# Cross-attention scores of two heads on the two row halves of the matmul array

## The reference, cut to what matters

```python
qh = (q @ Wq).reshape(b, l, HEADS, HEAD_DIM).transpose(0, 2, 1, 3)   # 16 heads of 64, l = 128
kh = (kv @ Wk).reshape(b, s, HEADS, HEAD_DIM).transpose(0, 2, 1, 3)  # s = 2048
vh = (kv @ Wv).reshape(b, s, HEADS, HEAD_DIM).transpose(0, 2, 1, 3)
qh = rms_norm(qh, q_norm_w)
kh = rms_norm(kh, k_norm_w)
scores = jnp.einsum('bhld,bhsd->bhls', qh, kh) * (1.0 / np.sqrt(HEAD_DIM))
scores = jnp.where(mask, scores, NEG_INF)
attn = jax.nn.softmax(scores, axis=-1)
o = jnp.einsum('bhls,bhsd->bhld', attn, vh)
```

## Time and profile before

| | us |
|---|---|
| runs shown: median (lowest to highest of 3) | 1441.21 (1439.97 to 1441.74) |
| profiled execution, its own time | 1442.03 |
| its span, first to last instruction | 1440.3 |
| cross attention, from its first context piece (76) to its last output (1002) | about 926 |
| mean granted clock of PE, share of full speed | 0.932 |

### The profile page before, as it was taken

How to read it: one execution, slowest core, us unless ns; L and a number is a source line. 1 busy time by engine, 2 the same in 40 slices (tenths; PEclk the granted TensorE clock), 3 DMA queues, 4 the chain that set the end, 5 groups by cost and what they waited for, 6 DMA issues and landing times. The chain is left out here.

```text
span 1440.3 us, 30819 instructions
## 1 busy us (share of the span) xinstructions
PE 1230.4 (85%) x11696; PEld 1025.7 (71%) x11696; DVE 870.4 (60%) x1880; ACT 743.7 (52%) x1222; POOL 821.5 (57%) x699
## 2 busy tenths in 40 slices
PE   4669999989999999999999999995798855479418
PEld 3548888878888888888888888873587744368316
DVE  5846555576555577555576555553767668587573
ACT  4534666666666667566666666564533331123550
POOL 3516777767777768777767777774501126276210
PEclk9889999999999999999999999996999977779759
DMA  5044667797766798767688767667510022032000
GB/s 177 30 125 85 116 117 120 129 186 130 117 115 118 119 187 155 115 114 119 121 177 144 116 119 121 114 117 152 193 45 1 1 96 88 1 88 59 0 0 30
DMA packets 427554, 149.68 MB, mean 104 GB/s; under 512 B 408208, under 2 KB 408208, under 8 KB 427280
## 3 DMA queue, kind: packets, MB, share of 16 engines
q1 hardware_dynamic: 427408, 147.71, 52.7%
HBM read 45.94 MB, written 1.05 MB: 33 GB/s over the span
## 5 line engine op out<-in xcount | busy, mean ns | idle before, releaser
L358 PE MATMUL pair<-wkv_hi,ctx_hi 128*128 128x256 f16 x2048 | 560.5, 274 | 14.7 <-DVE ctx_lo L541 14.7
L360 PE MATMUL pair<-wkv_hi,ctx_lo 128*128 128x256 f16 x2048 | 560.3, 274 | 0.0
L359 PE MATMUL pair<-wkv_lo,ctx_hi 128*128 128x256 f16 x2048 | 560.3, 274 | 0.0
L566 DVE CUSTOM_DVE_ANT_0 probs<-bank,mask 128x512 f32<-128x512 f32 x256 | 176.7, 690 | 291.3 <-PE bank L636 282.9
L487 POOL TENSOR_TENSOR k_rinv<-k_ms,half_neg 128x8 f32<-128x8 f32 x128 | 212.7, 1662 | 206.3 <-DVE k_ms L585 204.8
L477 POOL TENSOR_TENSOR p_parts<-probs,p_parts 128x512 f16<-128x512 f32 x256 | 291.9, 1158 | 49.2 <-ACT p_parts L522 48.7
L358 PEld LDWEIGHTS pair<-wkv_hi,ctx_hi 128*128 128x128 f16 x2048 | 200.9, 98 | 67.5 <-DVE ctx_lo L541 16.4
L359 PEld LDWEIGHTS pair<-wkv_lo,ctx_hi 128*128 128x128 f16 x2048 | 201.1, 98 | 50.0
L360 PEld LDWEIGHTS pair<-wkv_hi,ctx_lo 128*128 128x128 f16 x2048 | 201.1, 98 | 24.0
L526 ACT ACTIVATE k_lh<-k_n 128x512 f16<-128x512 f32 x128 | 80.5, 629 | 205.8 <-DVE k_n L591 205.2
L515 ACT ACTIVATE probs<-probs,neg_max 128x512 f32<-128x512 f32 x256 | 182.9, 714 | 1.3 <-DVE neg_max L575 1.1
(11 more groups left out here) (244 smaller groups left out, 2048.6 us busy)
## 6 DMA issues: line engine op xcount, KB each, us to landing
ctx_raw<-in_ctx_t_dram SPq DMA_DIRECT2D x64, 256.0 KB, 3.0
cross_out_raw<-in_w_qkv_dram SPq DMA_DIRECT2D x12, 512.0 KB, 4.2
pt<-p_parts SPq DMA_TRANSPOSE x256, 3.3
down_raw<-in_w_down_dram SPq DMA_DIRECT2D x12, 256.0 KB, 2.7
ffn_raw<-in_w_up_dram SPq DMA_DIRECT2D x12, 256.0 KB, 2.8
ffn_raw<-in_w_gate_dram SPq DMA_DIRECT2D x12, 256.0 KB, 2.6
w_raw<-in_wq_dram SPq DMA_DIRECT2D x4, 512.0 KB, 7.9
w_raw<-in_wk_dram SPq DMA_DIRECT2D x4, 512.0 KB, 4.8
```

The source lines that it names most:

```text
L358: nc.tensor.matmul(to, x_hi[k], w_hi[k], start=(k == 0), stop=False)
L359: nc.tensor.matmul(to, x_hi[k], w_lo[k], start=False, stop=False)
L360: mm = nc.tensor.matmul(to, x_lo[k], w_hi[k], start=False, stop=(k == n - 1))
L566: nc.vector.tensor_tensor_reduce(probs[n % PROBS][:, :], scores[:, :], mask[:, k, :], 1.0, LOWEST, ALU.add, ALU.max, chunk_max[head % 2][: ...
```

## The change

**Scores.** A pair of parts (one chunk, both heads) is now scored in one slot, every second slot. The keys of the first head stand on rows 0 to 63 and those of the second on rows 64 to 127, hi in the first half of `kt` and lo in the second; `q_st` is laid out in the same way. Each head takes three products (hi·hi, lo·hi, hi·lo; lo·lo, which was a by-product, is no longer made), each a matmul of 64 rows and 512 columns, the two heads in turn, each into a bank of its own (`bank[4]`, `bank[5]`). PE waits once for each pair until DVE has taken the last scores of both.

**PSUM.** `pair` has two tensors instead of three, so a projection waits for `k_n` and `v_lo` of the projection two before it. The outputs of the two heads have a bank each (`two`).

**Order and buffers.** The parts now alternate between the heads. The lags are 8, 17 and 20 instead of 10, 15 and 18; `kt` has 3 buffers instead of 6, `probs` 10 instead of 6, the small maxima 4 instead of 2.

**Prologue.** `stack` holds hi of eight heads and then lo of eight heads. Eight transposes for each unit, into two banks in turn, and one copy by DVE give `q_st`. The second set of transposes, ACT's copy and DVE's copy `hi2` are gone.

```diff
-SCORE_LAG, EXP_LAG, PV_LAG = 10, 15, 18
-CTX_RAWS, KTS, VS, PROBS, PTS = 2, 6, 11, 6, 3
+SCORE_LAG, EXP_LAG, PV_LAG = 8, 17, 20
+CTX_RAWS, KTS, VS, PROBS, PTS = 2, 3, 11, 10, 3
...
@@ -74,9 +74,11 @@
             of_stage[1].extend(handles)
             return handles
 
-        pair = [whole.enter_context(nc.psum_tensor(f"pair{i}", [P, 4, 256], F32)) for i in range(3)]
-        bank = [pair[i // 2][:, 2 * (i % 2):2 * (i % 2) + 2, :].rearrange("p a n -> p (a n)") for i in range(6)]
-        bank += [whole.enter_context(nc.psum_tensor(f"bank{i}", [P, 512], F32)) for i in (6, 7)]
+        pair = [whole.enter_context(nc.psum_tensor(f"pair{i}", [P, 4, 256], F32)) for i in range(2)]
+        bank = [pair[i // 2][:, 2 * (i % 2):2 * (i % 2) + 2, :].rearrange("p a n -> p (a n)") for i in range(4)]
+        bank += [whole.enter_context(nc.psum_tensor(f"bank{i}", [P, 512], F32)) for i in range(4, 6)]
+        two = whole.enter_context(nc.psum_tensor("two", [P, 2, 512], F32))
+        bank += [two[:, i, :] for i in range(2)]
 
...
-                    pe.wait_ge(hi2_done, m + 1)
-                    wait(pe, st_a, m)
-                    for h in range(HH):
-                        mm = nc.tensor.transpose(t_a[:, h * P:(h + 1) * P],
-                                                 stack[m % 2][:, h, 0:2, :].rearrange("p a d -> p (a d)"), ident16[:, :])
+                    wait(pe, st_a, m - 1)
+                    for i in range(HH):
+                        mm = nc.tensor.transpose(t_a[m % 2][:, i * P:(i + 1) * P],
+                                                 stack[m % 2][:, :, :, :].rearrange("p a h d -> p (a h d)")[:, i * P:(i + 1) * P],
+                                                 ident16[:, :])
                     mm.then_inc(tr_a, 1)
-                    wait(pe, st_b, m)
-                    for h in range(HH):
-                        mm = nc.tensor.transpose(t_b[:, h * P:(h + 1) * P],
-                                                 stack[m % 2][:, h, 1:3, :].rearrange("p a d -> p (a d)"), ident16[:, :])
-                    mm.then_inc(tr_b, 1)
...
-                wait(act, tr_b, m - 1)
-                nc.scalar.activation(stack[m % 2][:, :, 0, :], q_w[m % 2][:, :, :], ACT.Copy).then_inc(hi_done, 1)
-
-            def keep(m):
-                act.wait_ge(tr_b, m + 1)
-                nc.scalar.activation(q_st[:, unit(m)[2], 1, :, :].rearrange("p h q -> p (h q)"), t_b[:, :],
-                                     ACT.Copy).then_inc(st_b, 1)
+                wait(act, tr_a, m - 1)
+                nc.scalar.activation(stack[m % 2][:, 0, :, :], q_w[m % 2][:, :, :], ACT.Copy).then_inc(hi_done, 1)
...
-                wait(dve, tr_b, m - 1)
-                nc.vector.tensor_copy(stack[m % 2][:, :, 2, :], stack[m % 2][:, :, 0, :]).then_inc(hi2_done, 1)
-                nc.vector.tensor_tensor(stack[m % 2][:, :, 1, :], q_w[m % 2][:, :, :], stack[m % 2][:, :, 0, :],
+                nc.vector.tensor_tensor(stack[m % 2][:, 1, :, :], q_w[m % 2][:, :, :], stack[m % 2][:, 0, :, :],
                                         ALU.subtract).then_inc(lo_done, 1)
 
...
-        k_n = sb("k_n", [P, 2, TILES, HD], F32, c)
-        k_lh = [sb(f"k_lh{i}", [P, 2 * TILES, 2, HD], F16, c) for i in range(2)]
-        kt = [sb(f"kt{i}", [P, 2, CHUNK], F16, c) for i in range(KTS)]
+        k_n = sb("k_n", [P, TILES, 2, HD], F32, c)
+        k_lh = [sb(f"k_lh{i}", [P, 2, CHUNK], F16, c) for i in range(2)]
+        kt = [sb(f"kt{i}", [P, 2 * TILES, P], F16, c) for i in range(KTS)]
...
-        pair, scores = g["pair"], bank[6]
-        o_new = bank[7][:, 0:2 * VW].rearrange("p (h v) -> p h v", h=2)
+        pair, scores = g["pair"], bank[4:6]
+        o_new = g["two"][:, :, 0:VW]
...
-            return pair[d % 3][:, :, 0:2 * HD].rearrange("p t (h e) -> p h t e", h=2)
+            return pair[d % 2][:, :, 0:2 * HD].rearrange("p t (h e) -> p t h e", h=2)
 
         def v_of(d):
 
-            return pair[d % 3][:, :, 2 * HD:4 * HD].rearrange("p t (h e) -> p t h e", h=2)
+            return pair[d % 2][:, :, 2 * HD:4 * HD].rearrange("p t (h e) -> p t h e", h=2)
...
-                        wait(pe, k_n_done, d - 2)
-                        wait(pe, v_lo_done, d - 2)
+                        wait(pe, k_n_done, d - 1)
+                        wait(pe, v_lo_done, d - 1)
...
-                        sp.wait_ge(s_done, last_score(d - KTS))
-                    sp.dma_start_transpose(kt[d % KTS][:, :, :].rearrange("p h (t k) -> p (h t) k", t=TILES),
-                                           k_lh[d % 2][:, :, :, :].rearrange("p a b e -> p (a b e)")).then_inc(kt_in[d % 2], 16)
+                        sp.wait_ge(s_done, d - KTS + 1)
...
-                    dve.wait_ge(s_done, n + 1)
+                    dve.wait_ge(s_done, n // 2 + 1)
...
-                if (n := part(SCORE_LAG, slot)) is not None:
-                    u, h, k = n // 8, n // CHUNKS % 2, n % CHUNKS
-                    b, group, at = u // GROUPS, u % GROUPS, CHUNKS * u + k
+                if (n := part(SCORE_LAG, slot)) is not None and n % 2 == 0:
+                    u, at = n // 8, n // 2
+                    b, group = u // GROUPS, u % GROUPS
                     pe.wait_ge(kt_in[at % 2], 16 * (at // 2 + 1))
                     wait(pe, s_max_done, n)
-                    for i in range(2):
-                        mm = nc.tensor.matmul(scores[:, :], q_st[:, group // 4 * B + b, i, 2 * (group % 4) + h, :],
-                                              kt[at % KTS][:, h, :], start=(i == 0), stop=(i == 1))
+                    for i, (q_part, k_part) in enumerate(((0, 0), (1, 0), (0, 1))):
+                        for h in range(2):
+                            rows = slice(HD * h, HD * (h + 1))
+                            mm = nc.tensor.matmul(scores[h][:, :], q_st[rows, group // 4 * B + b, q_part, group % 4, :],
+                                                  kt[at % KTS][rows, TILES * k_part:TILES * (k_part + 1), :].rearrange(
+                                                      "p t k -> p (t k)"), start=(i == 0), stop=(i == 2))
                     mm.then_inc(s_done, 1)
```

More of the change, by code:

```diff
@@ L90, in program @@
         wkv_hi, wkv_lo = (sb(n, [P, KD, GROUPS, 4 * HD], F16, stage_q) for n in ("wkv_hi", "wkv_lo"))
-        q_st = sb("q_st", [P, UNITS, 2, HH, P], F16, stage_q)
+        q_st = sb("q_st", [P, UNITS, 2, HH // 2, P], F16, stage_q)
         prologue(nc, sems, sb, bank, locals())
@@ L136, in prologue @@
         q_n, q_w = ([xn[:, 2 * j + i, :].rearrange("p (h d) -> p h d", h=HH) for i in range(2)] for j in range(2))
-        stack = [sb(f"q_stack{i}", [P, HH, 3, HD], F16, c) for i in range(2)]
+        stack = [sb(f"q_stack{i}", [P, 2, HH, HD], F16, c) for i in range(2)]
         x_in, norm_in = sems(c, "x_in norm_in")
@@ L144, in prologue @@
             c, "qp_done sq_done raw_done ss_done ms_done rinv_done qn_done qw_done")
-        hi_done, hi2_done, lo_done, tr_a, tr_b, st_a, st_b = sems(
-            c, "hi_done hi2_done lo_done tr_a tr_b st_a st_b")
+        hi_done, lo_done, tr_a, st_a = sems(c, "hi_done lo_done tr_a st_a")
         q_st = g["q_st"]
-        t_a, t_b = (bank[4 + i].bitcast(F16) for i in range(2))
+        t_a = [bank[4 + i][:, :].bitcast(F16) for i in range(2)]
         block = c.enter_context(nc.Block())
@@ L268, in _ @@
                                      ACT.Copy).then_inc(x_hi, 1)
-            for n in range(UNITS + 4):
-                if n >= 4:
-                    keep(n - 4)
+            for n in range(UNITS + 2):
                 if n < UNITS:
@@ L327, in keep @@
                 dve.wait_ge(tr_a, m + 1)
-                nc.vector.tensor_copy(q_st[:, unit(m)[2], 0, :, :].rearrange("p h q -> p (h q)"),
-                                      t_a[:, :]).then_inc(st_a, 1)
+                nc.vector.tensor_copy(q_st[:, unit(m)[2], :, :, :].rearrange("p a h q -> p (a h q)"),
+                                      t_a[m % 2][:, :]).then_inc(st_a, 1)
             weights_lo(range(KD))
@@ L387, in cross_attention @@
         left = sb("left", [P, B, CHUNKS], F32, c)
-        chunk_max = [sb(f"chunk_max{i}", [P, CHUNKS], F32, c) for i in range(2)]
-        head_max = [sb(f"head_max{i}", [P, 1], F32, c) for i in range(2)]
-        neg_max = [sb(f"neg_max{i}", [P, 1], F32, c) for i in range(2)]
+        chunk_max = [sb(f"chunk_max{i}", [P, CHUNKS], F32, c) for i in range(4)]
+        head_max = [sb(f"head_max{i}", [P, 1], F32, c) for i in range(4)]
+        neg_max = [sb(f"neg_max{i}", [P, 1], F32, c) for i in range(4)]
         ctx_in = sems(c, " ".join(f"ctx_in{i}" for i in range(CTX_RAWS)))
@@ L552, in _ @@
                 if (n := part(SCORE_LAG + 1, slot)) is not None:
-                    head, k = n // CHUNKS, n % CHUNKS
+                    head, k, h = head_of(n), n % 8 // 2, n % 2
                     b = n // (8 * GROUPS)
-                    if n % (8 * GROUPS) < CHUNKS:
+                    if n % (8 * GROUPS) < 8 and h == 0:
```

(10 more changed lines are left out.)

35 lines of the change are left out of this document (15 added, 20 removed).

## The result

| | before | after |
|---|---|---|
| median of 16 runs each (lowest to highest), us | 1441.47 (1439.97 to 1445.48) | 1446.27 (1442.47 to 1449.17) |
| profiled execution: its own time / its span, us | 1442.03 / 1440.3 | 1448.14 / 1446.4 |

The ratio is 1.003, with a 95% interval from 1.002 to 1.0039: the changed kernel is slower, by 4.8 us by the medians (2.9 to 5.6 by the interval), where 1432 us and a faster kernel were forecast.

A forecast was written before the change was run, and what follows sets the result against it. PE issue was taken to bound cross attention's middle part. Terms -28.2 + 7.7 + 3.0 + 9.0 + 3.7 - 4.4 = -9.2 took 1442.03 to 1432.8, median 1432 us; own range 1419 to 1440, 8-in-10 range 1419 to 1470.

The forecast's parts named there:

- Scores, -28.2: Cross attention scores: three overlapped steps of 0.22 us a pair instead of four, saving 0.22 x 128 pairs = 28.2 us.
- The rival of loads that aren't hidden: Score matmuls: a half's next weight loads may have to wait, giving 1466 us, or 1449 at half that; chance 0.13.
- Changes of mode, 256 x 0.030 = +7.7: Between 128-row and 64-row matmuls around scores: two changes a pair, each costing one issue step of 0.030 us, +7.7 us.
- my bounds of 0 and 0.325 a pair: Cost of the row-mode changes around scores: from nothing to the pipeline running empty, 0.325 us a pair or 41.6 us.
- the 0.13 from which I said the sign turns: Row-mode changes around scores: from 0.13 us a pair on they decide, where the forecast's sum is zero.
- The rival of the empty array: Row-mode changes around scores: the array runs empty at each, 0.325 us a pair, +34 us, 1466 us; chance 0.23.
- Third buffer, start +3.0: Start of cross attention: with two projection buffers, PE is held behind DVE's late v_lo, +3.0 us.
- Third buffer, turns +9: Three turns of batch: with two projection buffers, twelve places hold PE longer behind a late DVE, +9 us.
- my lower end: Third buffer in the turns of batch: cost 0 if the load chain gets ahead when PE is held.
- The steady slack of 0.9: Steady slots of cross attention: DVE frees the projection buffer 0.9 us before PE wants it, so two buffers cost 0.
- Lags, +3.7: Drain after the last projection: two more parts are left, at 1.86 us each by the transposes' pace, +3.7 us.
- Prologue, -4.4: Prologue: second transposes and ACT's copy dropped, -3.1 us, and six DVE copies dropped, -1.3; together -4.4 (-2 to -7).

The follow-up runs named there:

- the f32 runs: Changed kernel with two small extra f32 identity matmuls ahead of each pair's scores, on half the rows each, then on all 128 rows: 1472.28 and 1487.34 us.

## Why the prediction was wrong, by its own steps

- **Scores, -28.2.** Right. A step of two matmuls takes as long as one (0.216), their starts 3 to 4 ns apart, so 128 steps of 0.2155 are 27.6 us saved. The rival of loads that aren't hidden is out: the steps are no longer than before, but for the 11 ns on the one behind a change. (Its estimate by the page has a slip: 0.20 a pair is 25.6 us, so 1458 and not 1450.) The Trainium skill, "TensorE: Matmul & The Clock Gate", section "Part 3: Packing small matmuls — row/col tiling", has tiles start 4 ns apart, and the trace agrees; the loss that its figure for four tiles implies does not show with two halves.
- **Changes of mode, 256 x 0.030 = +7.7.** This is the step that failed. I took the low row, transposes to f32 products without a gap, as the nearest. But both of its operations have the full 128 x 128 shape, and the f32 runs show that a change of type makes no gap and a change of shape does: the row was no instance of the thing. Measured, a change costs 0.093 to 0.097 as a gap and 0.011 on the step behind it, 0.106 in all: 256 x 0.106 = **+27.1**, 19.5 more than in the sum. The load does stay behind the change, as the prediction had it; what it had at one issue step of 0.030 is the pause. It is inside my bounds of 0 and 0.325 a pair, at 0.212, and above the 0.13 from which I said the sign turns. The rival of the empty array names the right place, but its price, the whole tails, is too high (+41.6; 1466): the pause is shorter than a tail. The Trainium skill, "TensorEngine Tiling (Array Packing)", section "Key Properties", says that a change of tiling drains the TensorE; the traces agree that each change costs, and give it a price that the page does not have. I had a rule against a row that wasn't of its kind, and followed the row.
- **Third buffer, start +3.0.** Right: 3.03.
- **Third buffer, turns +9.** Too much. The three turns, 26 slots each (from 14 ahead of the change of batch to 12 behind it), took 280.5 us in the changed kernel (280.3 and 279.7 in the other two with two buffers whose slots are of the same length), and 276.0, 276.8, 278.9 and 283.4 in the four with three: about +1.4 by the means, less than their spread, so it isn't told from nothing (and the +4.2 to +4.7 of the two buffers alone leaves 1.2 to 1.7 beside the start). PE's waits for `k_n` are 5.9 us in six places, but the waits behind late scores fell from 8.6 to 1.3 (four places), and that the load chain gains when PE is held, which I had named as my lower end, would fit, but no run takes it apart. The steady slack of 0.9 held: no steady pair waits.
- **Lags, +3.7.** About half. From the last projection to the last `o_acc` (to the copy's end) it is 38.97 us in the changed kernel, and 37.45 in the kernel before; with the four runs that share its lags (36.17 to 37.97) the mean is 37.0: +2.0. The queue does have two more transposes of parts behind the last projection, 17 against 15, and its long rows go at the pace I used (15 in 27.09 us, 1.81 each); but from the first of them to the last it takes 31.2 us against 29.0, so the two cost 2.2 and not 3.6. Why, I can't show.
- **Prologue, -4.4.** Right: -4.3 when taken alone, with an interval from -7.1 to -2.6. The profiled execution of the changed kernel hides half of it: its first projection is only 2.4 us earlier than that of the kernel before. In that execution a f32 product of the queries lasts 491 ns, in five others of the eight that share its prologue 441 to 450:

```profile
L345 PE MATMUL pair<-wq_hi,xt_hi 128*128 128x512 f32 x32 | 15.7, 491 | 2.9 <-DVE xt_lo L321 2.9
```

  The clock goes with it. Windows from 36 to 50 us, the changed kernel and then the one with the heads one by one, which has the same prologue:

```profile
36.00:50.00 14.00, 10.96 (x52) 8.66 (x53) 12.18 (x15) 6.79 (x10) 8.79 (x9) 0.74 0.24 76
36.00:50.00 14.00, 11.61 (x64) 8.89 (x63) 12.18 (x15) 7.88 (x12) 10.05 (x10) 0.89 0.21 73
```

  In this stretch the granted clock is 0.74 in the three executions with 475 to 497 ns, and 0.88 to 0.89 in the five others. Those five have their first projection at 71.7 to 72.2 us, the three at 74.4 to 75.1. The kernel before and its run with two buffers, at 0.89 and 0.88, have it at 77.5 and 79.8, so between executions at a like clock the gain is 5.3 us or more. Why the clock stays low for longer in some executions is open.

By the runs the sum is -27.6 + 27.1 + 3.0 + 1.4 + 2.0 - 4.3 = +1.6 us, where the medians differ by 4.8 and the interval reaches from 2.9 to 5.6. Its own uncertainty is some 3 us, since the two parts that were timed alone have intervals of that size. Part of the rest shows when the two profiled executions are taken stage by stage. Their spans differ by 6.1 us: -2.4 up to the first projection, +3.1 in the first eight slots, +1.6 in the turns, +0.8 in all other slots, +1.5 from the last projection to the last `o_acc`, +1.5 behind it. The +0.8 stands where the sum has -27.6 + 27.1 = -0.5: a pair is 0.003 longer than before and not 0.003 shorter, and the last pair's scores now stand whole ahead of the last projection slot (+0.4). The +1.5 at the end is spread: the common stages took 438.5 to 441.8 us in the five kernels with the old order and 438.7 to 441.4 in the eight with the new one, 439.9 and 440.3 in the mean.

The sign turns on the changes of mode: with 0.030 in place of 0.106 the same sum is -18. And that the measured time lies only 4.8 us above the kernel before is in part luck. With that term alone put right the prediction's sum would have been -9.2 + 19.5 = +10.3; the turns and the lags, together 9.3 us too high, hide much of the miss. Its wide range, to 1470, holds 1446 only because it was drawn up to the case of an empty array.

## What to carry to other kernels

Count changes of tile shape on the matmul engine as work: each cost 0.106 us here with f16, about as much as one full matmul of 256 columns (0.109), and a visit with narrow tiles needs two. Packing two heads on the two halves pays once a visit saves clearly more than 0.21 us, that is two or more steps of 512 columns; here it saved one. And when a cost is bounded by rows, ask of each row whether it is an instance of the thing: a row of another kind that shows nothing is no evidence for a low price.

## What the runs showed of the hardware that I had not expected

- The pause at a change of tile shape hardly moves: 93 ns from 128 x 128 to 64 x 128, 91 to 64 x 32 and to f32, 96 from 64 x 32 to 64 x 128 and 93 to 97 back to 128 x 128, with loads of 89 to 95 and of 182 to 186 ns behind it. From f32 to f16 in one shape there is none. The step behind the pause is 11 ns longer with f16 and 48 with f32.
- No weight load is pulled ahead over such a change: in the changed kernel the load behind it starts 4 to 5 ns ahead of its matmul, where it started 0.22 us ahead before.
- Matmuls on the two halves need not alternate in the program: three and three started in pairs as well, 10 ns apart instead of 3.
- A weight load of 32 columns lasts 89 ns and one of 128 columns 94.
